# Group attentions: the first batch's mask rows taken from SBUF, not from DRAM

## The chip, the cores and the metric

One NeuronCore of a Trainium2 chip runs one program, a stack of eight layers. The metric is the device time of one execution in microseconds (us); the median of several executions is quoted. The engines are named as the profile names them: PE (TensorE), ACT (ScalarE), DVE (VectorE), POOL (GpSimd) and SP (SyncE, which issues nearly all transfers).

## The reference, cut to what matters

Eight layers work on `x` of 16 batches x 256 tokens x 128 channels. The two that matter here are the sixth and the eighth, `_L1_ffn_ref`, the "group" attention, called twice with the same weights. Every token but the first five is put into one of two groups by its likeness to a guide, and it sees only the keys of its group and the first five:

```python
sim = (sim - sim.min()) / (sim.max() - sim.min())
pos = sim > 0.9
logits = jnp.einsum('bqhd,bkhd->bhqk', q * scale, k)
def masked_attn(tok_mask):
    key_mask = jnp.concatenate([jnp.ones((Bx, REG), bool), tok_mask], axis=1)
    l = jnp.where(key_mask[:, None, None, :], logits, -jnp.inf)
    a = jax.nn.softmax(l, axis=-1)
    return jnp.einsum('bhqk,bkhd->bqhd', a, v)
x_pos = masked_attn(pos)
x_neg = masked_attn(~pos)
tok_out = jnp.where(pos[:, :, None, None], x_pos[:, REG:], x_neg[:, REG:])
```

`sim.min()` and `sim.max()` go over all 4096 tokens. So no token's group is known before all tokens have been looked at: the masks of every batch come out at once, at the end of a stage of its own.

## The kernel before, in words

A batch is 256 tokens: `NT` = 2 tiles of 128 (`P`). There are `NB` = 16 batches, so 32 tiles (`TILES`), and 16 heads in 8 pairs (`PAIRS`).

**The two stages of a group layer.** `groups` finds the groups. While it runs, SP already carries out the first pieces of the attention that follows (`following.first`): the constant rows (`sp_first`) and the query and key parts of batches 0 and 1 (`HOSTED` = 2), which go from SBUF to `stack_dram` and from there into the stacks. The last thing `groups` does is to write `K.mask`, 128 partitions x 4 kinds x 32 tiles, on DVE. Then comes a barrier, and `narrow_attention`'s `run` starts its own block.

**The stacks.** `st` holds, for three batches in turn (`KEEP`), for queries (`which` = 0) and keys (`which` = 1), for each pair and each of 256 tokens, a column of numbers along the partitions: 48 rows of bf16 parts of q and k, then at `ROW_EXTRA` two mask rows, then three rows for the maxima. One head of a pair lies in partitions 0 to 63, the other in 64 to 127 (`z`). A product of a query column with a key column gives the score with its mask already added, since a query's mask rows hold 0 or -1e30 and a key's 0 or 1. The mask rows are the same for all pairs.

**How the masks get there.** PE transposes `K.mask` (line 1007), so that kind and tile run along the partitions; ACT copies the result to `mask_rows` (line 1169). Partition 32 * a + n holds kind a of tile n. SP writes all of it to `mask_dram` (line 942), waits until that has landed (semaphore `kept0`), and issues 16 transfers at line 956 (`sp_masks`): for batch 0 and 1, for each half of the pairs (`i`), for each `z` and each `which`, one transfer of 2 rows x 4 pairs x 256 tokens, 512 bytes per row and pair. The masks of batches 2 to 15 are read in the same way by four transfers each, before each half of the stack's load (line 984).

**Who waits.** The pieces of a batch are walked through in an order written out by hand (`NARROW_ORDER`), one list an engine. On PE a batch begins with the piece "max": four matmuls a pair (line 1068) give all the scores, and DVE takes their maximum (line 1281). For the first pair and the fifth, PE waits for the masks of that half (`masked`, at 64 = four transfers of 16) and for the stack's load (`landed`). "reg_scores" (lines 1142 and 1143) waits for the first half's masks too. The pieces "score" (line 1089), "value" (line 1109) and so on follow; for batch 0 they start when all eight maxima of the batch are there.

Of the kernel before, what the change touches and what calls it, by code (L numbers as in the profile page):

```python
# [12 lines left out]
P = 128  # L13
NB = 16
S = 256
NT = S // P
TILES = NB * NT
# [571 lines left out]
PAIRS = H // 2  # L589
# [186 lines left out]
HOSTED = 2  # L776
# [39 lines left out]
def narrow_attention(nc, K, kind, name, W):  # L816
# [9 lines left out]
    ROW_EXTRA = PARTS * D8  # L826
# [11 lines left out]
    with ExitStack() as ctx:  # L838
        ctx.enter_context(nc.cleanup_on_exit())

        def sb(n, shape, dt=F32):
# [3 lines left out]
            "stat_dve", "var_ready", "rstd_ready", "norm_ready", "first_dve", "first_var", "first_rstd", "first_norm",  # L845
            "weights", "set_pe", "set_act", "set_pool", "kept0", "kept1", "rows",
            "xn", "full0", "full1", "drained0", "drained1",
            "rotated", "summed", "part", "parted0", "parted1", "landed00", "landed01", "landed10", "landed11", "masked00", "masked01", "masked10", "masked11", "pool_own", "dve_own",
            "maxima", "maxed", "joined", "split", "shifted0", "shifted1", "spread0", "spread1",
            "scored", "exps", "valued", "taken", "biased", "added", "stats",  # L850
            "reg_q", "reg_v", "reg_max", "reg_sum", "reg_new", "reg_probs", "reg_out")}
# [4 lines left out]
        masked = [s["masked00"], s["masked01"], s["masked10"], s["masked11"]]  # L856
# [7 lines left out]
        st = sb("st", [P, KEEP, 2, PAIRS, S], BF16)  # L864
# [74 lines left out]
        def sp_setup(sp):  # L939
            if kind == "group":  # L940
                sp.wait_ge(s["set_act"], 1)
                sp.dma_start(K.mask_dram.rearrange("a n p -> (a n) p"), mask_rows[:]).then_inc(s["kept0"], 16)

            for b in range(HOSTED if kind == "group" else 0):
                for i in range(2):
                    sp_masks(sp, b, i)

        def sp_masks(sp, b, i):
            half = slice(i * PAIRS // 2, (i + 1) * PAIRS // 2)
            if b == 0:  # L950
                sp.wait_ge(s["kept0"], 16)
            for z in range(2):
                at = slice(64 * z + ROW_EXTRA, 64 * z + ROW_EXTRA + 2)
                for which in range(2):
                    src = K.mask_dram[2 * which:2 * which + 2, NT * b:NT * b + NT, :].rearrange("a n p -> a (n p)")
                    sp.dma_start(st[at, b % KEEP, which, half], src.unsqueeze(1).to_broadcast([2, PAIRS // 2, S])
                                 ).then_inc(masked[2 * i + b % 2], 16)
# [65 lines left out]
        def pe_piece(pe, what, i, b):  # L1023
# [27 lines left out]
            elif what == "max":  # L1051
# [3 lines left out]
                        pe.wait_ge(s["weights"], 1)  # L1055
                        wait(pe, s["set_act"], {"slope": 1, "group": 1, "rope": 2}[kind])
                if i % (PAIRS // 2) == 0:
                    if kind == "group":
                        pe.wait_ge(masked[2 * (i // (PAIRS // 2)) + b % 2], 64 * (b // 2 + 1))
                    pe.wait_ge(landed[b % 2][i // (PAIRS // 2)], LANDED * (b // 2 + 1))  # L1060
                wait(pe, s["maxed"], PAIRS * b + i - (1 if b == 0 else 0))
                Mx = max_bank(i, b)
# [58 lines left out]
            elif what == "turnmax":  # L1121
                pe.wait_ge(s["split"], b + 1)
                for t in range(NT):
                    ins = pe.transpose(bank[0:48].bitcast(BF16)[:, t * P:(t + 1) * P],  # L1124
                                       cols[:, b % 2, t].rearrange("p r z j -> p (r z j)"), K.ident16[:])
                ins.then_inc(full[m], 1)
            elif what == "attn":
                for k in ("turn0", "turn1"):
                    pe.wait_ge(drained[fill[k, b][0]], fill[k, b][1])
                for t in range(NT):  # L1130
                    ins = pe.transpose(bank[:, t * P:(t + 1) * P], att[:, b % 2, t, :], K.ident[:])
                ins.then_inc(full[m], 1)
            elif what == "project":
                pe.wait_ge(drained[fill["attn", b][0]], fill["attn", b][1])
                for t in range(NT):
                    ins = pe.matmul(bank[:, t * C:(t + 1) * C], att_t[:, b % 2, t * P:(t + 1) * P], W["out"], start=True, stop=True)  # L1136
                ins.then_inc(full[m], 1)
            elif what == "reg_scores":
                pe.wait_ge(s["reg_q"], b + 1)
                pe.wait_ge(landed[b % 2][0], LANDED * (b // 2 + 1))  # L1140
                pe.wait_ge(masked[b % 2], 64 * (b // 2 + 1))
                pe.matmul(bank[0:RH, 0:S], qblk[:, b % 2, :], qk[:, b % 2, 1, :], start=True, stop=False)
                pe.matmul(bank[0:RH, 0:S], K.not_first[0:ROW_SHIFT, :], st[0:ROW_SHIFT, b % KEEP, 1, 0, :], start=False,
                          stop=True).then_inc(full[m], 1)
            elif what == "reg_turn":
                pe.wait_ge(s["reg_probs"], b + 1)
                for t in range(NT):
                    ins = pe.transpose(bank[:, t * RH:(t + 1) * RH], pxn[:, t * P:(t + 1) * P], K.ident[0:RH, 0:RH])  # L1148
                ins.then_inc(full[m], 1)
            elif what == "reg_value":  # L1150
                pe.wait_ge(drained[fill["reg_turn", b][0]], fill["reg_turn", b][1])
                pe.wait_ge(s["reg_v"], b + 1)
                for t in range(NT):
                    ins = pe.matmul(bank[:, 0:RH], vplain[:, t, :], pxt[:, t * RH:(t + 1) * RH],  # L1154
                                    start=(t == 0), stop=(t == NT - 1))
                ins.then_inc(full[m], 1)
# [1494 lines left out]
```

## Time and profile before

| | |
|---|---|
| median of 3 runs | 2233.96 us (2232.46 to 2238.82) |
| the profiled execution, its own time | 2238.64 us |
| its span, first to last instruction | 2236.9 us |
| mean granted TensorE clock | 0.944 of full speed |
| busy: PE, DVE, ACT, POOL | 88%, 69%, 52%, 36% of the span |
| first group layer's attention: mask write issued, first maxima | 1582.49 us, 1587.15 us |
| second group layer's attention: the same | 1957.06 us, 1961.09 us |

The span leaves out what lies before the first and after the last instruction (1.7 us here). The profile is one execution, and this one was among the slower; a difference of two of its times is more to be trusted than the sum. "Landing" of a transfer is the moment at which its semaphore has its full count; "issue" is the time that SP spends on it.

### The profile page before, as it was taken

The page shows a single profiled execution, that of the slowest core. Times are in us where ns is not written, and L with a number is a line of the kernel's source. Part 1 is how long each engine was busy: PE and PEld are TensorE (multiplying, and loading weights), DVE is VectorE, ACT ScalarE, POOL GpSimd, SP SyncE. Part 2 cuts the span into 40 slices and gives each one's busy share as a digit, 9 for nine tenths or more (in the row PEclk, how much of TensorE's full clock was granted, in tenths as well). Part 3 has the DMA queues.
Part 4 walks back from the last instruction along what each step waited for, and adds up shares of the span by engine and source line. Part 5 has one row for each costly group of instructions (what it writes and reads, how often), then busy time and mean ns, then how long its engine had stood idle before and what let it go on. Part 6 is the DMA issues. An engine that isn't in the chain of part 4 may idle for free. (4 is left out here: it accounts for less than half of the span.)

```text
span 2236.9 us, 54582 instructions
## 1 busy us (share of the span) xinstructions
PE 1978.6 (88%) x21591; PEld 1310.0 (59%) x21591; DVE 1550.5 (69%) x2798; ACT 1169.8 (52%) x1966; POOL 797.7 (36%) x1306
## 2 busy tenths in 40 slices
PE   5999999999989997999799979997599985479996
PEld 2666666666668884665588856664255542335553
DVE  5787868777876336667663367774689966779994
ACT  4444444444333324666433236666388875458874
POOL 4444544545432212343322134430333414333340
PEclk9999999999999997999899989998699997779998
DMA  6000000000013343443122524440334410224431
GB/s 175 1 1 1 2 1 1 2 1 2 2 35 70 88 106 85 122 113 96 37 64 66 127 72 116 119 109 6 94 112 115 111 48 0 58 77 108 118 110 51
DMA packets 163151, 146.71 MB, mean 66 GB/s; under 512 B 15264, under 2 KB 131376, under 8 KB 160852
## 3 DMA queue, kind: packets, MB, share of 16 engines
q1 hardware_dynamic: 162900, 143.22, 25.1%
q8 instruction: 175, 2.87, 0.6%
q14 instruction: 76, 0.62, 0.1%
HBM read 88.64 MB, written 54.52 MB: 64 GB/s over the span
## 5 line engine op out<-in xcount | busy, mean ns | idle before, releaser
L1281 DVE TENSOR_REDUCE l_group_mx<-maxima 128x4 f32<-128x1024 f32 x248 | 304.0, 1226 | 53.5 <-PE maxima L1068 51.9
L1206 ACT ACTIVATE l_group_pr<-scores 128x1024 f32<-128x1024 f32 x256 | 261.6, 1022 | 70.4 <-PE scores L1089 67.9
L2482 POOL TENSOR_TENSOR l_wide_tiles_sum<-l_wide_pr 128x256 f32<-128x256 f32 x256 | 180.9, 727 | 200.2 <-ACT l_wide_pr L2421 200.0
L2451 DVE RECIPROCAL l_wide_rc<-bank 128x256 f32<-128x256 f32 x128 | 224.0, 1750 | 5.3 <-PE bank L2378 3.8
L2421 ACT ACTIVATE l_wide_pr<-scores 128x512 f32<-128x512 f32 x256 | 139.0, 595 | 160.3 <-PE scores L2361 160.3
L2435 DVE TENSOR_REDUCE l_wide_mx<-maxima 128x2 f32<-128x512 f32 x248 | 159.3, 685 | 44.3 <-PE maxima L2341 44.1
L1281 DVE TENSOR_REDUCE l_slope_mx<-maxima 128x6 f32<-128x768 f32 x124 | 119.0, 959 | 67.9 <-PE maxima L1075 66.5
L2411 ACT ACTIVATE l_wide_qk<-bank 128x512 f32<-128x512 f32 x128 | 76.4, 597 | 155.4 <-PE bank L2325 155.4
L1281 DVE TENSOR_REDUCE l_rope_mx<-maxima 128x6 f32<-128x768 f32 x124 | 118.8, 958 | 45.1 <-PE maxima L1075 44.1
L1206 ACT ACTIVATE l_slope_pr<-scores 128x768 f32<-128x768 f32 x128 | 103.5, 809 | 74.4 <-PE scores L1096 74.3
L1109 PE MATMUL bank<-l_group_pr,va 128*32 128x256 f32 x2048 | 142.4, 397 | 0.0
L2372 PE MATMUL bank<-l_wide_pr,l_wide_va 128*64 128x256 f32 x1024 | 138.0, 390 | 2.5 <-DVE l_wide_att_t L2452 2.4
L1206 ACT ACTIVATE l_rope_pr<-scores 128x768 f32<-128x768 f32 x128 | 103.8, 811 | 66.1 <-PE scores L1096 65.9
L2361 PE MATMUL scores<-l_wide_qk 64*128 64x256 f32 x1024 | 131.4, 376 | 0.0
L1068 PE MATMUL maxima<-l_group_st 50*128 50x256 bf16 x992 | 101.6, 285 | 25.6 <-DVE l_group_mx L1281 15.2
L2477 POOL CAST l_wide_qk<-l_wide_qk 128x512 bf16<-128x512 f32 x128 | 78.1, 610 | 122.0 <-ACT l_wide_qk L2411 121.9
L1089 PE MATMUL scores<-l_group_st 53*128 53x256 bf16 x1024 | 102.4, 279 | 16.5 <-ACT l_group_pr L1206 11.7
L1379 POOL CAST l_group_cols<-l_group_mx 128x32 bf16<-128x32 f32 x32 | 6.7, 209 | 303.5 <-DVE l_group_mx L1281 303.5
L2361 PEld LDWEIGHTS scores<-l_wide_qk 64*128 64x128 f32 x1024 | 98.6, 189 | 9.8
L2372 PEld LDWEIGHTS bank<-l_wide_pr,l_wide_va 128*64 128x64 f32 x1024 | 63.3, 136 | 48.3 <-issue 21.7
L1929 ACT ACTIVATE l_rope_e_ht<-maxima 128x512 f32<-128x512 f32 x64 | 38.0, 595 | 96.6 <-PE maxima L1876 96.6
L1929 ACT ACTIVATE l_slope_e_ht<-maxima 128x512 f32<-128x512 f32 x64 | 38.0, 595 | 93.9 <-PE maxima L1876 93.9
(584 smaller groups left out, 4681.5 us busy)
## 6 DMA issues: line engine op xcount, KB each, us to landing
l_group_st<-stack_dram SPq DMA_DIRECT2D x128, 192.0 KB, 3.4
l_slope_st<-stack_dram SPq DMA_DIRECT2D x64, 192.0 KB, 4.0
l_rope_st<-stack_dram SPq DMA_DIRECT2D x64, 192.0 KB, 4.1
stack_dram<-l_group_parts SPq DMA_DIRECT2D x64, 192.0 KB, 2.3
l_slope_e_unit_prob<-prob_dram SPq DMA_DIRECT2D x16, 512.0 KB, 7.3
l_rope_e_unit_prob<-prob_dram SPq DMA_DIRECT2D x16, 512.0 KB, 7.5
stack_dram<-l_group_parts SPq DMA_DIRECT2D x64, 128.0 KB, 1.9
stack_dram<-l_slope_parts SPq DMA_DIRECT2D x32, 192.0 KB, 2.4
```

Of the source, the lines that this page charges most:

```text
L1068: ins = pe.matmul(Mx[:, z, first:first + keys], st[at, b % KEEP, 0, i, t * P:(t + 1) * P], st[at, b % KEEP, 1, i, 0:keys], start=(t == 0 o ...
L1089: ins = pe.matmul(Tp[:, z, t * S:t * S + S - first], st[at, b % KEEP, 1, i, t * P:(t + 1) * P], st[at, b % KEEP, 0, i, first:S], start=(t ...
L1109: ins = pe.matmul(Ob[i // 2][32 * z:32 * z + 32, (i % 2) * S + first:(i % 2) * S + S], va[:, b % KEEP, t, h // G, :], pr[:, (h // 2) % AHE ...
L1206: act.activation(pr[:, i % AHEAD, :, 0:keys], Tp[:, :, 0:keys], ACT.Exp).then_inc(s["exps"], 1)
L1281: dve.tensor_reduce(mx[:, b % 2, :, :, i], max_bank(i, b)[:, :, 0:BLOCKS * keys].rearrange("p z (a k) -> p z a k", k=keys), AX.X, ALU.max, ...
L2361: ins = pe.matmul(Tb[z][:, t * S:(t + 1) * S], qk[rows(z), at, i, 1, t * P:(t + 1) * P], qk[rows(z), at, i, 0, :], start=False, stop=(t == ...
L2372: ins = pe.matmul(Ob[i % 2][rows(z), 0:S], va[:, at, kt, 2 * i + z, :], pr[:, i % 2, z, kt * S:(kt + 1) * S], start=(kt == 0), stop=(kt == ...
L2421: act.activation(pr[:, i % 2, z, :], Tb[z][:], ACT.Exp).then_inc(s["exps"], 1)
L2435: dve.tensor_reduce(mx[:, at, :, 2 * i + z], max_banks(i, b)[z][:].rearrange("p (t k) -> p t k", k=S), AX.X, ALU.max, negate=True).then_in ...
L2451: own.done(dve.reciprocal(rc[:], Ob[i % 2][:, S:2 * S]))
L2477: pool.tensor_copy(qk16[:, at, i], qk[:, at, i]).then_inc(s["half"], 1)
L2482: pool.tensor_tensor(tiles_sum[:, i % 2, z, :], pr[:, i % 2, z, 0:S], pr[:, i % 2, z, S:2 * S], ALU.add).then_inc(s["added"], 1)
```

## The change

For batch 0 alone, the mask rows no longer go by way of `mask_dram`. Eight transfers read `mask_rows` in SBUF and write the stack in SBUF: for each `z`, each `which` and each of the two tiles `t`, one of 2 rows x 8 pairs x 128 tokens, 256 bytes per row and pair. They are issued right behind the write to `mask_dram`, without a wait between. Only then does SP wait for `kept0`, and issue the eight reads for batch 1. A new semaphore `masked` counts the eight transfers; PE waits for all of them (128 = 8 x 16) ahead of the first pair of batch 0, where it waited for four reads, and at the fifth pair and in "reg_scores" too. The counts expected on the old semaphores fall by one turn for the even batches. The write to `mask_dram` stays, and batches 1 to 15 read as before.

```diff
-            "rotated", "summed", "part", "parted0", "parted1", "landed00", "landed01", "landed10", "landed11", "masked00", "masked01", "masked10", "masked11", "pool_own", "dve_own",
+            "rotated", "summed", "part", "parted0", "parted1", "landed00", "landed01", "landed10", "landed11", "masked00", "masked01", "masked10", "masked11", "masked", "pool_own", "dve_own",
...
                 sp.dma_start(K.mask_dram.rearrange("a n p -> (a n) p"), mask_rows[:]).then_inc(s["kept0"], 16)
-
-            for b in range(HOSTED if kind == "group" else 0):
+                for z in range(2):
+                    for which in range(2):
+                        for t in range(NT):
+                            row, at = 64 * z + ROW_EXTRA, 2 * which * TILES + t
+                            sp.dma_start(st[row:row + 2, 0, which, :, t * P:(t + 1) * P],
+                                         mask_rows[at:at + TILES + 1:TILES, :].unsqueeze(1).to_broadcast([2, PAIRS, P])).then_inc(s["masked"], 16)
+                sp.wait_ge(s["kept0"], 16)
                 for i in range(2):
-                    sp_masks(sp, b, i)
+                    sp_masks(sp, 1, i)
 
         def sp_masks(sp, b, i):
             half = slice(i * PAIRS // 2, (i + 1) * PAIRS // 2)
-            if b == 0:
-                sp.wait_ge(s["kept0"], 16)
...
                 if i % (PAIRS // 2) == 0:
-                    if kind == "group":
-                        pe.wait_ge(masked[2 * (i // (PAIRS // 2)) + b % 2], 64 * (b // 2 + 1))
+                    if kind == "group" and b == 0:
+                        pe.wait_ge(s["masked"], 128)
+                    elif kind == "group":
+                        pe.wait_ge(masked[2 * (i // (PAIRS // 2)) + b % 2], 64 * (b // 2 + b % 2))
...
-                pe.wait_ge(masked[b % 2], 64 * (b // 2 + 1))
+                if b == 0:
+                    pe.wait_ge(s["masked"], 128)
+                else:
+                    pe.wait_ge(masked[b % 2], 64 * (b // 2 + b % 2))
```

The order of SP's instructions at the start of the first group attention, before. A name in brackets is that of the first user of a semaphore that several layers share: `rows_turned` is here the signal that `mask_rows` is there, `rows_kept` is `kept0`.

```order
L1536 UNCONDITIONAL_BRANCH
L1495 UNCONDITIONAL_BRANCH [waits barrier_Pool_Activation_PE_DVE_SP_release]
L942 DMA mask_dram<-l_group_mask_rows 128x128 [waits rows_turned]
L956 DMA l_group_st<-mask_dram 2x4x256 [waits rows_kept]
L956 DMA l_group_st<-mask_dram 2x4x256 x3
L956 DMA l_group_st<-mask_dram 2x4x256 [waits rows_kept]
L956 DMA l_group_st<-mask_dram 2x4x256 x11
L991 DMA shift_dram<-l_group_rows 48x256 [waits l0_wide_exps]
```

And the same place in the changed kernel:

```order
L1544 UNCONDITIONAL_BRANCH
L1503 UNCONDITIONAL_BRANCH [waits barrier_Pool_Activation_PE_DVE_SP_release]
L942 DMA mask_dram<-l_group_mask_rows 128x128 [waits rows_turned]
L947 DMA l_group_st<-l_group_mask_rows 2x8x128 x8
L959 DMA l_group_st<-mask_dram 2x4x256 [waits rows_kept]
L959 DMA l_group_st<-mask_dram 2x4x256 x7
L994 DMA shift_dram<-l_group_rows 48x256 [waits l0_wide_exps]
```

The wait for the write stood ahead of the first transfer that PE needs; now it stands behind all those that PE needs for batch 0. The number of transfers is 17 both times. The second group layer has the same two pieces, and on the other engines no instruction changes its place.

## Rows read from the trace of the kernel before

**Rows 1.** The page: busy time of PE, and the granted clock in 40 slices.

```profile
PE 1978.6 (88%) x21591; PEld 1310.0 (59%) x21591; DVE 1550.5 (69%) x2798; ACT 1169.8 (52%) x1966; POOL 797.7 (36%) x1306
PEclk9999999999999997999899989998699997779998
```

**Rows 2.** The chain that ended last, second group layer: start us, us, what.

```profile
1957.06 1.55 DMA mask_dram<-l_group_mask_rows
...
1958.63 0.23 SPq L956
...
1959.50 1.35 DMA l_group_st<-mask_dram
1960.85 0.25 issue
1961.09 0.62 PE maxima L1068 x4
```

**Rows 3.** Timeline of the first group layer: start, us, engine, line, operation, count [idle before].

```profile
1582.49 0.34 SPq L942 DMA_DIRECT2D mask_dram<-l_group_mask_rows  x1
...
1584.69 4.75 SPq L956 DMA_DIRECT2D l_group_st<-mask_dram  x16
...
1587.15 0.61 PE L1068 MATMUL maxima<-l_group_st 50*128 50x256 bf16 x4 [4.99 <-DMA l_group_st<-mask_dram]
```

**Rows 4.** Source views of lines 942 and 956: durations ns min/median/max, first and last start; landing.

```profile
L942 SPq DMA_DIRECT2D mask_dram<-l_group_mask_rows x2: 337/338/338, 1582.5 to 1957.1; - x2
DMA to landing us min/median/max: 1.6/1.9/2.2
L956 SPq DMA_DIRECT2D l_group_st<-mask_dram x256: 230/259/367, 1584.7 to 2181.3; - x128
  PE maxima L1068: 9.4, 2
```

**Rows 5.** Transfers in a window: 1957.85 to 1958.40 (the mask write; slices of 13.75 ns).

```profile
DMA  0000366579999776542210000000000000000000
DMA packets 145, 0.03 MB, mean 60 GB/s; under 512 B 145, under 2 KB 145, under 8 KB 145
q1 hardware_dynamic: 145, 0.03, 27.4%
```

**Rows 6.** The same for 1585.4 to 1592 (the 16 mask reads of the first layer).

```profile
DMA packets 160, 0.07 MB, mean 10 GB/s; under 512 B 32, under 2 KB 160, under 8 KB 160
q1 hardware_dynamic: 160, 0.07, 3.4%
```

**Rows 7.** The same for 1954 to 1957 (batch 1's stack loads).

```profile
DMA packets 387, 0.69 MB, mean 231 GB/s; under 512 B 48, under 2 KB 48, under 8 KB 387
q1 hardware_dynamic: 387, 0.69, 91.6%
```

**Rows 8.** Timeline of the second group layer: SP's other transfers, and batch 1's first maxima.

```profile
1944.25 1.74 SPq L984 DMA_DIRECT2D l_group_st<-stack_dram  x4
...
1952.84 1.74 SPq L984 DMA_DIRECT2D l_group_st<-stack_dram  x4
...
1958.63 4.76 SPq L956 DMA_DIRECT2D l_group_st<-mask_dram  x16
...
1973.49 0.61 PE L1068 MATMUL maxima<-l_group_st 50*128 50x256 bf16 x4 [0.59 <-DVE l_group_mx L1281]
...
1975.58 0.32 SPq L991 DMA_DIRECT2D shift_dram<-l_group_rows  x1
```

**Rows 9.** Busy time in stretches: PE, PEld, DVE, ACT, POOL (count), PEclk, DMA share, GB/s.

```profile
1577.00:1587.00 10.00, 0.84 (x3) 0.59 (x3) 1.87 (x10) 2.32 (x4) 1.51 (x5) 0.50 0.37 90
1600.00:1614.00 14.00, 10.28 (x67) 4.42 (x65) 10.07 (x13) 4.88 (x8) 5.24 (x9) 0.50 0.45 110
2000.00:2100.00 100.00, 97.38 (x1097) 53.07 (x1089) 89.89 (x152) 81.28 (x121) 38.88 (x76) 1.00 0.42 114
```

**Rows 10.** Landing of the stack loads (line 984): min/median/max.

```profile
DMA to landing us min/median/max: 2.8/3.8/5.5
```

## The prediction

> **What bounds the kernel now.** The page comes first [rows 1]: PE is busy for 88% of the span, and its clock was granted nearly in full except in a few slices. A change of some small transfers can therefore count only where PE stands still. The chain of waits of the second group layer says where that is [rows 2]: the reader is to see that the write of the masks to DRAM, one issue after another of the reads at line 956, and the landing of the fourth read follow each other with nothing beside them, and that PE's first four maxima start 0.24 us after that landing. The timeline of the first group layer shows the same stretch [rows 3], and the source view of line 956 puts 9.4 us of PE's idle time down to these transfers, in two waits [rows 4]. (Part of those waits is time before the masks were written; only what follows line 942 is in play.) From the issue of the write to the first maxima it is 1587.15 - 1582.49 = 4.66 us in the first layer and 1961.09 - 1957.06 = 4.03 us in the second. These 8.7 us are all that the change touches, 0.39% of 2238.64 us. About 0.3%, or 6.7 us, is what a measurement of this kernel can tell from no change, so a clear gain would need three quarters of the whole stretch.
>
> **The parts of the stretch before.** Second layer [rows 2]: the write is issued at 1957.06 and has landed at 1958.61; the first read starts at 1958.63, 1.57 us after the write's issue. The fourth read, the last that PE needs, starts at 1959.50, 0.87 us later. It lands 1.35 us after its issue, and PE starts 0.24 us on. 1.57 + 0.87 + 1.35 + 0.24 = 4.03. First layer [rows 3]: 2.20 us to the first read. The 16 issues take 4.75 us, 0.297 us each, so the fourth starts 3 x 0.297 = 0.89 us later, and from there to PE's start it is 1587.15 - 1584.69 - 0.89 = 1.57 us (1.35 + 0.24 = 1.59 in the other layer).
>
> **Term 1, the wait for the write goes.** The first direct transfer can be issued when SP has done the write's issue: 0.34 us [rows 4] and the 0.05 us that lies between two issues (the pitch of 0.297 less some 0.24 of issue). So it starts 0.39 us behind the write where the first read started 1.57 or 2.20 us behind it: -1.18 us in the second layer, -1.81 us in the first.
>
> **Term 2, PE needs eight transfers where it needed four.** The old split by halves of the pairs let PE start on the first four reads. The new split is by tile, and a transfer carries all eight pairs; PE waits for all eight. Four more issues at 0.297 us: +1.19 us in each layer. The issue of this form, SBUF to SBUF, stands in no row. The nearest are the mask reads, 0.230 to 0.367 us [rows 4], and the mask write, 0.34 us; with the gap a pitch of 0.28 to 0.42 us. I keep 0.297, because the new transfers have the reads' two partitions and much the same count of pieces. Over the seven pitches the ends are -0.1 and +0.9 us a layer.
>
> **Term 3, the landing of the last one.** A read's pieces: 160 packets in the window of 16 reads, 10 each, 8 of 512 bytes and two small ones [rows 6]; 3.4% of 16 engines over 6.6 us is 3.6 us, or 22 ns a packet. The write was 128 pieces of 256 bytes and some 16 small ones, one for each engine; 27.4% of 16 engines over 0.55 us is 2.4 us, or 17 ns for each of 145 [rows 5]. Two small packets a read then mean two engines. A direct transfer has 16 pieces of 256 bytes and two small ones, 18 x 17 = 0.30 us of engine time, 0.15 us on each of two engines. That is half the pitch of the issues: the eight do not pile up, and the last one's landing is that of a single transfer. For it I take the read's 1.35 us, because it too ends in SBUF; difference 0. The ends: a write's first packet stands at 1957.89, 0.84 us after its issue (the first busy slice is the fourth of 13.75 ns [rows 5]), and with 0.15 us of pieces nothing shown excludes a landing after 1.0 us, -0.35 us a layer; the slowest small transfer here landed after 2.2 us [rows 4], +0.85 us a layer.
>
> On a transfer's fixed cost the two sources differ. The rows have 1.35 us for the read, 1.55 and 2.20 for the write. The Trainium skill ("DMA: Bandwidth & Descriptors", section "Anatomy of one DMA", written for transfers that GpSimd issues) gives each a fixed 2.0 us or so. By it the removed wait would be 2.0 us in both layers, so that each gains 2.0 - 0.39 - 1.19 = 0.42 us and the estimate for both is -0.84 us.
>
> **Edits that cost nothing, and their cover.** Batch 1's eight reads are issued behind the direct ones, from 2.77 us after the write (the write has landed by then in both layers) to about 5.1 us after it; before, SP was through at 1963.39, 6.3 us after [rows 8]. Batch 1's maxima begin at 1973.49, and SP's next transfer at 1975.58, so ten microseconds cover them; without that cover a late mask would hold PE by its own landing, 1.35 us. The fifth pair of batch 0 and "reg_scores" find `masked` full. The stack loads of batch 0 were issued from 1944.25 and those of batch 1 from 1952.84 [rows 8]; they land in 5.5 us at most [rows 10], so the first is no hidden second wait at 1961, and the direct transfers, whose first packet would come at 1957.06 + 0.39 + 0.84 = 1958.3, hardly meet the second. What is late next, if the masks came at once, is the copy of `mask_rows` itself, outside the stretch. The changed counts on `masked00` and its kin ask for the same transfers. The one new semaphore costs no instruction that waits.
>
> **What carries to the end.** Up to 1614 the granted clock is 0.50, half of 2.4 GHz, from before the wait on, and PE and DVE are busy 10.3 and 10.1 of 14 us, handing to one another [rows 9]; later PE is busy 97 of 100 us. Nothing in between has a fixed time to wait for, so a start that is earlier ends earlier by as much. I put nothing for the clock: the half clock begins long before this stretch and outlasts it.
>
> **The sum.** First layer -1.81 + 1.19 + 0 = -0.62 us. Second layer -1.18 + 1.19 + 0 = +0.01 us. Together -0.6 us: 2238.64 becomes 2238.0. The profiled execution was 4.7 us over the median of the runs, 2233.96; on that median the forecast is **2233.4 us**. With the ends of terms 2 and 3 it is between -0.6 - 0.2 - 0.7 = -1.5 and -0.6 + 1.8 + 1.7 = +2.9 us.
>
> **The rivals.**
>
> *The write's 2.20 us was chance, and nothing is gained.* The forecast's gain stands on that one wait. In the second layer the same write took 1.55 us, and there the four issues added eat what the wait removed gives. If an ordinary execution has 1.57 in both, the sum is 0.0 us, 2234.0. For it: nothing in the program makes the two layers differ. Against it: one landing in two is slow.
>
> *The fixed cost of 2.0 us.* As a mechanism here: every write to DRAM takes what the first layer's nearly took, so both layers gain. With 2.20 in both by the row, 2 x -0.62 = -1.2 us, 2232.7. Against it: the second layer's 1.55. Either way far inside 0.3%.
>
> *Slower: the small pieces set the pace.* The place is the two engines' queues, between the first direct transfer and the eighth. If a piece took what one took in the stack loads, 91.6% of 16 x 3 us over 387 packets, 114 ns [rows 7], a transfer would hold its engines for 9 x 0.114 = 1.02 us. The last would land 0.39 + 0.84 + 8 x 1.02 + 0.45 after the write's issue (0.45: the write's last packet at 1958.16 [rows 5], its landing at 1958.61), and PE start at 10.1 us where it started at 4.03 and 4.66: +6.1 and +5.4, together +11.5 us, 2245.5. It begins to cost from 0.297 / 9 = 33 ns a piece, and from about 80 ns it would show as slower by 0.3%. Against it: pieces of 256 bytes out of SBUF took 17 ns, pieces into these partitions 22 ns. The Trainium skill ("DMA: Bandwidth & Descriptors", "Specifications") says that below 512 bytes the transfer engines read, modify and write, which speaks against the new pieces, half as long as the old ones; it has no factor. Its section "Why small descriptors are slow (HBM only)" excepts SBUF to SBUF. No row here shows that kind of transfer.
>
> *The change does not do what it says.* PE would have to be held by something else at that point. The chain names the masks and the other conditions are met earlier, so I give it nothing of its own; it would read as no change.
>
> **How the numbers follow.** Forecast -0.6 us with its ends: 0.74. Nothing gained: 0.15. Both writes slow: 0.04. Small pieces set the pace: 0.03. The program's code and semaphore numbers shift elsewhere and move something by more than the runs scatter: 0.04, of which 0.02 faster, 0.01 slower, 0.01 within. Faster by over 0.3%: 0.02. Slower by over 0.3%: 0.03 + 0.01 = 0.04. Within 0.3%: 0.94. The runs shown lie from 2232.46 to 2238.82, ten times the effect. The range takes the lowest with the best end, 2232.46 - 1.5 = 2231.0, and the highest with the forecast, 2238.82 - 0.6 = 2238.2, which holds the median with the dearest end too (2236.9).
>
> **What would show it.** In the changed profile: eight transfers at line 947, each issued in 0.23 to 0.34 us, the first 0.39 us behind the write; PE's first maxima 4.0 to 4.1 us behind the write in both layers, the wait put down to the direct transfers; batch 1's reads through about 5.1 us behind it. Term 1 is wrong if SP stands still between line 942 and 947. Term 2 is wrong if the eight take other than 2.4 us. Term 3 is wrong if PE starts other than 1.6 us after the eighth's issue. The carry is wrong if the first maxima move and the end of the layer does not move with them. The whole is wrong if the median leaves the range.

## The result, and the profile after

The changed kernel took 2240.08 us (median of 20 runs, 2236.72 to 2243.57), the kernel before 2235.45 us (20 runs, 2232.46 to 2238.82). The ratio is 1.0020, 95% interval 1.0014 to 1.0026: 3.1 to 5.8 us slower. That is less than 0.3%, as forecast, but 2240.08 lies above the range given, and the sign is not that of the forecast of -0.6 us. On the median of the kernel before that stood beside it, 2235.45, the forecast would have been 2234.8. The profiled execution took 2240.27 us, with a span of 2238.6 us.

The page of the changed kernel has the same instruction counts and the same clock in each slice as [rows 1]:

```profile
PE 1980.8 (88%) x21591; PEld 1312.3 (59%) x21591; DVE 1549.3 (69%) x2798; ACT 1169.5 (52%) x1966; POOL 797.2 (36%) x1306
PEclk9999999999999997999899989998699997779998
```

The chain that ended last, second group layer (start us, us, what), answers to [rows 2]:

```profile
1956.72 0.34 SPq L942
...
1957.11 0.57 SPq L947
...
1961.13 1.66 DMA l_group_st<-l_group_mask_rows
1962.79 0.25 issue
1963.04 0.62 PE maxima L1073 x4
```

The write's landing is gone from the chain, and the first direct transfer starts 0.39 us behind the write, as the forecast had it. But one issue now takes 0.52 us (the first one 0.57) and not 0.26, and eight of them stand in a line. The first group layer shows the same in its timeline (start, duration, engine, line, count), against [rows 3]:

```profile
1580.35 0.34 SPq L942 DMA_DIRECT2D mask_dram<-l_group_mask_rows  x1
1580.74 4.66 SPq L947 DMA_DIRECT2D l_group_st<-l_group_mask_rows  x8
...
1585.45 2.54 SPq L959 DMA_DIRECT2D l_group_st<-mask_dram  x8
...
1586.80 0.61 PE L1073 MATMUL maxima<-l_group_st 50*128 50x256 bf16 x4 [6.79 <-DMA l_group_st<-l_group_mask_rows]
```

The source views (durations in ns min/median/max) put the two kinds of transfer side by side; [rows 4] has 230/259/367 for the reads of before:

```profile
L947 SPq DMA_DIRECT2D l_group_st<-l_group_mask_rows x16: 522/523/673, 1580.7 to 1961.1; - x16
...
  PE maxima L1073: 13.4, 2
...
L959 SPq DMA_DIRECT2D l_group_st<-mask_dram x240: 230/258/492, 1585.4 to 2182.2; - x120
```

PE waited 13.4 us for the direct transfers ahead of its first maxima in the two layers, where it had waited 9.4 us for the reads [rows 4]: +4.0 us. The packets in the window from 1958.2 to 1963.0 of the changed kernel, nearly all of them the direct transfers', answer to [rows 5] and [rows 6]:

```profile
DMA packets 164, 0.04 MB, mean 8 GB/s; under 512 B 156, under 2 KB 164, under 8 KB 164
q1 hardware_dynamic: 164, 0.04, 3.5%
```

3.5% of 16 engines over 4.8 us is 2.7 us, 16 ns a packet. The small pieces are as quick as they were read off [rows 5]; the transfer engines have nothing to do most of this time.

**Where the time is.** Take as the stretch what lies between PE's transposition of the masks and PE's first maxima, since nothing else is changed. Before, the transpositions of line 1007 stand in the timeline at

```profile
1581.89 0.26 PE L1007 MATMUL scores<-ident,mask 128*128 128x128 bf16 x1 [4.32 <-PEq L1536]
1956.45 0.27 PE L1007 MATMUL scores<-ident,mask 128*128 128x128 bf16 x1 [4.30 <-PEq L1536]
```

and in the changed kernel at

```profile
1579.75 0.26 PE L1010 MATMUL scores<-ident,mask 128*128 128x128 bf16 x1 [4.31 <-PEq L1544]
1956.12 0.26 PE L1010 MATMUL scores<-ident,mask 128*128 128x128 bf16 x1 [4.31 <-PEq L1544]
```

With the starts of the maxima in [rows 3] and [rows 2], the stretches were 5.26 and 4.64 us; they are 7.05 and 6.92 us. The sum rose from 9.90 to 13.97 us, by 4.07. What lies between and behind the stretches stayed: from the first layer's first maxima to the second layer's transposition it is 369.30 us before and 369.32 us after, from the second layer's first maxima to the end of the span 275.8 and 275.6. What was added there came out at the end in full. The two spans differ by only 1.7 us because the changed kernel's execution came to its first transposition 2.14 us earlier. That part of the program is the same, and the six variants below reached it between 1576.7 and 1580.9 us, so this is scatter between executions and no effect of the change.

### The profile page after: what moved, and what is told of

Read it like the earlier page. It is cut to its first block and busy times, and to the rows that moved or that the text cites. A ratio compares the mean times of both kernels' runs of the same rounds, so it can differ in the third digit from the quotient of the medians.

```text
span 2238.6 us, 54582 instructions
## 1 busy us (share of the span) xinstructions
PE 1980.8 (88%) x21591; PEld 1312.3 (59%) x21591; DVE 1549.3 (69%) x2798; ACT 1169.5 (52%) x1966; POOL 797.2 (36%) x1306
```

## The experiments

In the table, a stretch is as above, read from the trace of each kernel, and the ratio is that of the run times to the kernel before, measured beside it.

| kernel | stretch, layers 1 and 2, us | sum less before's | ratio (95%) |
|---|---|---|---|
| before | 5.26, 4.64 | | |
| changed | 7.05, 6.92 | +4.1 | 1.0020 (1.0014 to 1.0026) |
| same eight shapes, read from DRAM | 6.53, 6.21 | +2.8 | 1.0012 (0.9997 to 1.0027) |
| write issued behind the eight | 6.64, 6.57 | +3.3 | 1.0011 (0.9997 to 1.0025) |
| four direct transfers | 5.74, 5.64 | +1.5 | 1.0009 (1.0000 to 1.0018) |
| four direct, on two queues | 4.27, 4.03 | -1.6 | 0.9999 (0.9990 to 1.0008) |
| four DRAM reads, on two queues | 5.70, 4.56 | +0.4 | 1.0003 (0.9994 to 1.0011) |
| eight direct, on two queues | 5.46, 5.17 | +0.7 | 1.0007 (0.9998 to 1.0016) |

The ratios of the six variants do not by themselves tell one from no change (0.1% is 2.2 us, and each interval is about as wide as that to either side). They run in the order of the stretches, near enough; the stretches are what the verdicts below rest on. How far these scatter is seen in the three probe kernels below, which hold the kernel before's own program: from the write's issue to the first maxima their sums over the two layers are 8.9, 9.0 and 9.1 us, where the kernel before has 8.7. Where the write is waited for, a difference of 0.4 us in the sum therefore tells nothing.

**The same shapes from DRAM.** The eight transfers read `mask_dram` behind the wait for the write:

```diff
+                sp.wait_ge(s["kept0"], 16)
+                from_dram = K.mask_dram.rearrange("a n p -> (a n) p")
...
-                                         mask_rows[at:at + TILES + 1:TILES, :].unsqueeze(1).to_broadcast([2, PAIRS, P])).then_inc(s["masked"], 16)
-                sp.wait_ge(s["kept0"], 16)
+                                         from_dram[at:at + TILES + 1:TILES, :].unsqueeze(1).to_broadcast([2, PAIRS, P])).then_inc(s["masked"], 16)
```

> The changed kernel with its eight transfers in the same shapes, but read from mask_dram behind the wait for the write. Theory A (SBUF on both sides costs the issue): issues of 0.26 to 0.28 us, pitch 0.30; PE's first maxima 1.57 to 2.2 + 7 x 0.30 + 1.6 = 5.3 to 5.9 us behind the write's issue; 1.2 us a layer more than the kernel before, +2.4 us in all, ratio to before 1.001. Theory B (the shape costs): issues of 0.52 us, pitch 0.57, first maxima 7.5 to 8.1 us behind the write, +6.8 us in all, ratio 1.003.

Measured, in the source view of that kernel:

```profile
L949 SPq DMA_DIRECT2D l_group_st<-mask_dram x16: 231/263/265, 1583.3 to 1960.1; - x16
```

and in its chain, the last read and its landing:

```profile
1960.11 1.38 DMA l_group_st<-mask_dram
```

The issue is 0.263 us with the same 16 pieces of 256 bytes, the same destination and the same repeats. First maxima stood 1586.99 - 1581.07 = 5.92 and 1961.73 - 1956.12 = 5.61 us behind the write's issue. So the shape is not what costs; what changed is that the source lies in SBUF. The run also measures term 2 alone: it has the kernel before's issue and landing, and eight transfers to wait for instead of four. From the first read's issue to the first maxima it took 3.73 and 3.72 us, where the kernel before took 2.46 in both layers, so four more reads cost 1.26 us a layer. The rest of the +2.8 us is a write that landed 0.3 us later in the second layer.

**The write behind the eight.** Only the line of the write is moved:

```diff
-                sp.dma_start(K.mask_dram.rearrange("a n p -> (a n) p"), mask_rows[:]).then_inc(s["kept0"], 16)
                 for z in range(2):
...
+                sp.dma_start(K.mask_dram.rearrange("a n p -> (a n) p"), mask_rows[:]).then_inc(s["kept0"], 16)
                 sp.wait_ge(s["kept0"], 16)
```

> The changed kernel with the write to mask_dram issued behind the eight direct transfers instead of ahead of them. Theory (the eight issues are the path, one behind the other): the first maxima 7 x 0.57 + 1.66 + 0.25 = 5.9 us behind the first direct issue, so 0.39 us a layer less than the changed kernel, 0.8 us in all; issues still 0.52 us. Rival (the direct transfers are slow because they share the engines with the write just issued, whose landing rose from 1.6 or 2.2 to 2.2 or 2.4 us): issues fall to 0.26 us and the landing to 1.35, first maxima about 3.7 us behind the first direct issue, 2.6 us a layer less than the changed kernel.

The source view:

```profile
L946 SPq DMA_DIRECT2D l_group_st<-l_group_mask_rows x16: 522/523/672, 1581.5 to 1960.6; - x16
```

and the landing of the last direct transfer in the chain:

```profile
1960.56 1.69 DMA l_group_st<-l_group_mask_rows
```

The issues are unchanged, so the write that is still under way does not slow them. First maxima 6.04 and 5.96 us behind the first direct issue; 0.76 us less than the changed kernel's stretches in sum, as the 0.39 us a layer had it.

**Which forms are dear.** The kernel before with small transfers added at its end, ahead of the store of the result; the program's own work is untouched, and nothing it reads later is written. Three transfers of a form, to different places, then a wait. Each figure below rests on three issues in one execution:

```python
for n, r in enumerate((16, 48, 112)):
    sp.dma_start(landing[r:r + 2, :, 0:P], source[0:33:32, 0:P].unsqueeze(1).to_broadcast([2, PAIRS, P])).then_inc(probed, 16)
settle()
```

> The kernel before, and at its end, ahead of the store of the result, 13 forms of small transfer on SP, three of each to different rows or columns, each three waited for: (1) the old mask read, DRAM to SBUF, 2 x 4 x 256; (2) 2 x 8 x 256; (3) the new form's shape from DRAM; (4) the new form itself, SBUF to SBUF, rows 32 partitions apart, 128 elements repeated 8 times; (5) with adjacent rows; (6) with 4 repeats; (7) 8 repeats of 256 elements; (8) 4 repeats of 256; (9) one piece of 128 a row, no repeat; (10) 8 different pieces of 128; (11) one run of 2048 a row; (12) 128 partitions of 128; (13) SBUF to DRAM, 2 rows of 128. The source of the probes is a tile of zeros. Theory A (SBUF on both sides is what costs; the run from DRAM in the same shape had issues of 0.263 us where the direct ones have 0.523): (4) to (12) all about 0.5 us, (1) to (3) 0.26, (13) 0.25 to 0.34. Theory A2 (SBUF on both sides costs by the piece): (9) 0.28, (6) and (8) 0.39, (4) 0.52, (12) far over 0.52. Theory C (the step of 32 partitions): (5), (10), (11) and (12) 0.26 to 0.34, (4) and (6) to (9) 0.5. Landing after the end of an issue: about 1.1 us for all of 2 rows.

The source views, for (1), (4), (5), (8), (9) and (13) in this order, as ns min/median/max:

```profile
L2637 SPq DMA_DIRECT2D landing<-mask_dram x3: 236/252/253, 2223.7 to 2224.3; - x3
L2646 SPq DMA_DIRECT2D landing<-source x3: 522/555/686, 2229.7 to 2231.0; - x3
L2649 SPq DMA_DIRECT2D landing<-source x3: 622/633/680, 2232.7 to 2234.1; - x3
L2658 SPq DMA_DIRECT2D landing<-source x3: 523/523/523, 2241.5 to 2242.6; - x3
L2661 SPq DMA_DIRECT2D landing<-source x3: 472/492/514, 2244.3 to 2245.4; - x3
L2673 SPq DMA_DIRECT2D mask_dram<-source x3: 248/253/254, 2256.2 to 2256.8; - x3
```

Every transfer from SBUF to SBUF is at 0.47 us or above, one single piece a row too; the others have medians of 0.25 to 0.27. (12), with 128 pieces, has a median of 0.60, and (7), with twice the bytes of (4), 0.52. So neither the number of pieces nor the bytes are what costs (theory A2), and neither is the step of 32 partitions: adjacent rows, (5), are dearer still.

**Which sides.**

> The kernel before, and at its end 13 more forms on SP, three of each: (1) two rows of 128 from DRAM to DRAM; SBUF to SBUF with one piece of 128 a row: (2) one row, same partition, (3) one row from a partition 8 on, (4) two rows, same partitions, (5) to (9) two rows whose sources lie 2, 8, 16, 32, 64 partitions apart, (10) step 8 on both sides; (11) DRAM to two rows 8 partitions apart; (12) 16 rows, SBUF to SBUF; (13) 16 rows from DRAM. Theory A (an issue is dear when both sides are SBUF; in the run of forms before, 0.49 to 0.66 us for all nine of those and 0.25 to 0.27 for the DRAM ones): (2) to (10) and (12) 0.45 to 0.66, (1), (11), (13) 0.25 to 0.30. Theory D (an issue is cheap when the sides are of unlike kind): (1) 0.5 too. The source's step decides only within 0.49 to 0.66.

Theory A held for the SBUF to SBUF forms (0.47 to 0.68 us) and fell with the others; theory D has (1) right and falls with (11). The source views for (1), (5), (11), (12) and (13):

```profile
L2637 SPq DMA_DIRECT2D mask_dram<-mask_dram x3: 544/582/583, 2224.9 to 2226.1; - x3
L2649 SPq DMA_DIRECT2D landing<-source x3: 563/563/563, 2236.7 to 2237.9; - x3
L2667 SPq DMA_DIRECT2D landing<-mask_dram x3: 541/552/552, 2252.8 to 2254.0; - x3
L2670 SPq DMA_DIRECT2D landing<-source x3: 541/585/588, 2255.7 to 2256.9; - x3
L2673 SPq DMA_DIRECT2D landing<-mask_dram x3: 336/417/420, 2258.6 to 2259.5; - x3
```

DRAM to DRAM is as dear, and so is DRAM to two rows that lie 8 partitions apart.

**Controls.**

> The kernel before, and at its end 13 forms on SP, three of each. In the run of sides before this one, a transfer from DRAM to two rows 8 partitions apart took 0.54 us to issue and DRAM to DRAM 0.58, so that 'both sides in SBUF' is not the whole of it. In order: (1) DRAM to two adjacent rows, one piece of 128 each; (2) the same to rows 8 apart; (3) to rows 8 apart with 8 repeats; (4) SBUF to DRAM from two adjacent rows; (5) from rows 8 apart; (6) from rows 32 apart; (7) DRAM to one row; (8) DRAM to 16 rows; (9) the old mask read, 2 x 4 x 256; (10) the new direct form; (11) the old read again; (12) DRAM to DRAM; (13) the old read again. Theory E (cheap, 0.25 to 0.34, is only a transfer with exactly one side in SBUF and its partitions adjacent): (1), (4), (7), (8), (9), (11), (13) cheap; (2), (3), (5), (6), (10), (12) 0.47 to 0.6. Theory F (one piece a row is dear, a repeated one cheap, when the other side is DRAM): (1), (2), (7) dear and (3), (9) cheap. Theory G (it is the place in the program or what was issued before): (9), (11) and (13) differ.

The source views for (2), (4), (5), (6), (8), (9) and (12):

```profile
L2640 SPq DMA_DIRECT2D landing<-mask_dram x3: 541/576/687, 2230.9 to 2232.3; - x3
L2646 SPq DMA_DIRECT2D mask_dram<-source x3: 235/247/257, 2237.1 to 2237.7; - x3
L2649 SPq DMA_DIRECT2D mask_dram<-source x3: 542/567/622, 2238.7 to 2240.0; - x3
L2652 SPq DMA_DIRECT2D mask_dram<-source x3: 452/467/467, 2241.6 to 2242.6; - x3
L2658 SPq DMA_DIRECT2D landing<-mask_dram x3: 312/415/418, 2245.8 to 2246.6; - x3
L2661 SPq DMA_DIRECT2D landing<-mask_dram x3: 241/254/261, 2248.3 to 2248.9; - x3
L2670 SPq DMA_DIRECT2D mask_dram<-mask_dram x3: 584/585/589, 2255.1 to 2256.3; - x3
```

Theory E sorts all of them. (3) and (10) were dear with 0.59 and 0.52 us, (1), (7), (11) and (13) cheap with 0.25 to 0.26. The one that it has slightly wrong is (8): 16 rows from DRAM cost 0.42, more than 0.34. It makes the direct form of the change dear for two reasons, either of which would do: both sides lie in SBUF (adjacent rows do not help, (5) of the first probes), and the source rows are stepped (they cost 0.47 towards DRAM too, (6) here). Theory F falls with (1) and (3), theory G with (9), (11) and (13), which agree while dear forms stand between them. Why a stepped row or a second side in SBUF costs some 0.3 us of issue is not shown by any run; nor why two rows 32 or 64 partitions apart come at 0.47 to 0.49 and rows 1 to 16 apart at 0.56 to 0.62.

**Four direct transfers.** The masks are turned by two transpositions so that a batch's two tiles lie in one row of 256:

```diff
+                for t in range(NT):
+                    ins = pe.transpose(Tp[0:4 * NB, 0, :].bitcast(BF16)[:, t * P:(t + 1) * P],
+                                       K.mask[:].rearrange("p a (b t) -> p t (a b)", t=NT)[:, t, :], K.ident16[:])
...
+                        row, at = 64 * z + ROW_EXTRA, 2 * which * NB
+                        sp.dma_start(st[row:row + 2, 0, which],
+                                     mask_rows[at:at + NB + 1:NB, :].unsqueeze(1).to_broadcast([2, PAIRS, S])).then_inc(s["masked"], 16)
```

> The masks are turned so that both tiles of a batch lie in one row (two transposes instead of one, 64 rows of 256 columns), and batch 0 takes four direct transfers of 2 rows x 8 pairs x 256 instead of eight of 128. Theory A (each direct issue costs 0.52 us, pitch 0.57, whatever its piece count): four in 2.3 us, the first maxima 0.39 + 3 x 0.57 + 1.66 + 0.25 = 4.0 us behind the write's issue, 2.3 us a layer less than the changed kernel, and some 0.15 us later to the write for the second transpose and the longer copy; against the kernel before -0.6 + 0 + 0.3, so ratio 1.000, and against the changed kernel 4 us less. Theory A2 (by the piece or the byte): the issue rises to 0.6 us or more, and the gain shrinks.

The first maxima came 4.91 and 4.81 us behind the write, not 4.0. In the source view:

```profile
L946 SPq DMA_DIRECT2D l_group_st<-l_group_mask_rows x8: 622/624/807, 1578.1 to 1954.7; - x8
```

and in the chain:

```profile
1954.65 1.92 DMA l_group_st<-l_group_mask_rows
```

The write's issue rose to 0.47 and 0.52 us, an issue to 0.62, the landing to 1.92. The dearer issue is not theory A2's price by the byte, since (7) of the first probes, the same pieces at a step of 32, had 0.52; its rows are 16 partitions apart, and in the probes such a step cost 0.08 us more than one of 32 (0.562 against 0.487). The landing, from the end of the issue, is 1.30 us; in the probes (7), also of 8 KB, landed 1.3 us behind the end of its last issue and (4), of 4 KB, 1.1 us. Half the transfers took 2.6 us off the two stretches, of 4 us expected; it still does not reach the kernel before.

**Four direct ones on two queues.** As the last, but SP issues the two of the lower partitions, ahead of the write, and ACT those of the upper ones:

```diff
+                act.wait_ge(s["set_act"], 1)
+                for which in range(2):
+                    row, at = 64 + ROW_EXTRA, 2 * which * NB
+                    act.dma_start(st[row:row + 2, 0, which],
+                                  mask_rows[at:at + NB + 1:NB, :].unsqueeze(1).to_broadcast([2, PAIRS, S])).then_inc(s["masked"], 16)
```

> As the last, but the two direct transfers of the upper partitions are issued by ACT right behind its copy of the mask rows, and SP issues its two ahead of the write to mask_dram. Theory (the path is: so many issues one behind the other, then one landing): first maxima 1 x 0.57 + 1.66 + 0.25 = 2.5 us behind the first direct issue, where the kernel before has 4.03 and 4.66 behind the write: 1.5 and 2.2 less, less 0.15 each for transpose and copy, -3.3 us in all, ratio 0.9985. ACT's later work (two activations and a table load, 2.1 us, wanted 4.5 us after the first maxima) hides its 1.2 us of issues. Rival (two queues' transfers hold one another up on the same engines, or an issue from ACT costs more): first maxima later than 3.5 us, ratio 0.9995 or above.

The chain, second layer:

```profile
1954.96 0.69 SPq L945
...
1955.70 2.21 DMA l_group_st<-l_group_mask_rows
...
1958.16 0.63 PE maxima L1074 x4
```

The chain of the second layer shows one issue where there were four or eight, and a landing of 2.21 us where 1.66 was expected. The first maxima came 3.4 and 3.2 us behind the first issue, not 2.5, though earlier than the rival's 3.5. Both things that the rival names are there in part: an issue from ACT took 0.63 to 1.25 us, and the ratio is where it put it, above 0.9995. The stretches are 5.7 us shorter than the changed kernel's and 1.6 us shorter than the kernel before's; the run time beats the changed kernel's (0.9990 to 1.0008 against 1.0014 to 1.0026) and is not told apart from the kernel before's.

**Eight direct ones on two queues.** The changed kernel's own transfers, four issued by SP behind the write, four by ACT:

```diff
+                act.wait_ge(s["set_act"], 1)
+                first_masks(act, 1)
...
-                for z in range(2):
+                first_masks(sp, 0)
```

> The changed kernel with its eight direct transfers shared out: SP issues its four behind the write, ACT the other four behind its copy of the mask rows. Nothing else is changed. Theory (it is the line of eight issues that holds PE): first maxima 0.39 + 3 x 0.57 + 1.66 + 0.25 = 4.0 us behind the write, 2.3 us a layer less than the changed kernel, -4.6 us in all: ratio to the kernel before 1.000. Rival (the direct transfers themselves, or their piling up on two engines, hold PE): 6 us and ratio 1.002 as with eight on one queue.

The stretches fell by 3.3 us in sum, of 4.6 expected; the first maxima stood 4.86 and 4.57 us behind the write. The transfers, their shapes, their number and the two sides are those of the changed kernel. Only the line of issues is halved, and with it goes most of what was lost (3.3 of 4.1 us). What falls short of the 4.6 stands in the chain, as the landing of the last one, and in the source view of ACT's issues:

```profile
1958.50 2.09 DMA l_group_st<-l_group_mask_rows
...
L943 ACTq DMA_DIRECT2D l_group_st<-l_group_mask_rows x8: 533/670/1140, 1581.5 to 1958.1; - x8
```

**Four DRAM reads on two queues.** Batch 0's four reads carry all pairs; SP and ACT issue two each behind the wait for the write:

```diff
+        def first_masks(eng, z):
+            for which in range(2):
+                row = 64 * z + ROW_EXTRA
+                src = K.mask_dram[2 * which:2 * which + 2, 0:NT, :].rearrange("a n p -> a (n p)")
+                eng.dma_start(st[row:row + 2, 0, which], src.unsqueeze(1).to_broadcast([2, PAIRS, S])).then_inc(s["masked"], 16)
```

> The masks of batch 0 by way of DRAM again, as four reads with all eight pairs each (2 x 8 x 256), two issued by SP and two by ACT, both behind the wait for the write. Theory (path = write's landing, issues in a line, one landing): 1.57 to 2.2 + 1 x 0.30 + 1.38 + 0.25 = 3.5 to 4.1 us from the write's issue to the first maxima, 0.55 us a layer less than the kernel before; -1.1 us in all, ratio 0.9995, which is about as good as the direct form on two queues (ratio 0.9999) without a direct transfer. Rival: an issue from ACT is dearer, as it was for the direct ones (0.63 to 1.25 us), and nothing is gained.

The chain, second layer:

```profile
1953.73 0.23 SPq L943
...
1954.01 1.96 DMA l_group_st<-mask_dram
```

A miss: nothing is gained. The issues are as cheap as before, also from ACT (median 0.260 us, one of four at 0.56), but the last landing takes 1.96 us where one queue had 1.35 to 1.38. That rise eats the 0.6 us of issues saved: from the first read's issue to the first maxima it is 2.55 and 2.49 us, where it was 2.46. (The other 0.3 us of the +0.4 is the write, which landed after 2.55 us in the first layer.) Some 0.15 us of the rise belong to the form, twice as large: in the probes, on one queue, (2) landed 1.26 us behind the end of its last issue and (1) 1.11 us. A later landing stands in all three kernels with two queues; no run shows its cause.

## Why the prediction was wrong, point by point

- **What bounds it, and what is in play**: right. The stretch behind line 942 is all that moved.
- **Term 1, the wait for the write goes**: right to the hundredth. The first direct transfer started 0.39 us behind the write in both layers.
- **Term 2, eight transfers at the pitch of 0.297 us**: this is the step that failed. Eight instead of four was right, and the run with the DRAM source confirms the price of four more reads (1.26 us a layer, 1.19 forecast). From the first direct issue to the eighth it took 1961.13 - 1957.11 = 4.02 us in the second layer, not 2.08, which is a pitch of 0.574 us, and 0.1 us more in the first layer, where the eight issues took 4.66 us in all: +2.0 us a layer. The error was to choose the nearest rows by partitions and pieces and to pass over what no row shared: a source and a destination both in SBUF, and source rows 32 partitions apart. The dearest end, 0.42 us, was taken from the same rows of transfers with one side in DRAM, so it was no bound.
- **Term 3, the landing**: forecast 1.35 us from the issue, measured 1.66. It is the same error again. From the end of an issue it is 1961.13 + 0.52 to 1962.79, 1.14 us, where before it was 1959.50 + 0.26 to 1960.85, 1.09 us. The landing was right; the issue inside it was too short by half.
- **The sum**: with 0.39, 4.02 and 1.66 + 0.25 in the place of 0.39, 2.08 and 1.59, the second layer takes 6.32 us from the write, which is what the chain shows; the first took 6.45. Against 4.03 and 4.66 the sum is +4.1 us instead of -0.6, beyond the dearest end that the prediction gave, +2.9. The medians differ by 4.6, with an interval of 3.1 to 5.8.
- **The slower rival, small pieces**: it had the sign but not the mechanism. The packets took 16 ns, the engines were idle in between, and the queues did not pile up. The Trainium skill ("DMA: Bandwidth & Descriptors", section "Why small descriptors are slow (HBM only)") excepts transfers between SBUF and SBUF from the penalty for small pieces; by that exception, the trace agrees as far as the pieces go, with those 16 ns.
- **The 2.20 us as chance**: wrong. In the kernels that wait for the write it landed after 2.20, 2.19 and 2.55 us in the first layer and after 1.57, 1.89 and 1.47 in the second (issue to next issue, in the kernel before, in the one with eight DRAM reads and in the one with four on two queues). The three kernels with probes hold the kernel before's own program up to the probes, and have 2.26, 2.41 and 2.22 against 1.55, 1.47 and 1.85. The reason stays open, but the layer alone is not it: where the write was issued later, the layers agree (1.52 and 1.53 us behind the eight, 2.02 and 2.00 with four direct ones on two queues). The transfers of the kernel before from 1582.49 to 1584.69 show one thing that only the first layer has: one packet of 8 KB on the queue that the profile calls instruction, which took some 0.5 us (1.4% of 16 engines over 2.2 us). Nine packets of the write, as many as one engine has of it, start 1.3 to 1.5 us behind the write's issue, and all others by 1.1, as in the second layer. Such a packet stands beside the write in the first layer of all nine kernels that issue it right behind the copy, and in the second layer of none. In the second layer the landing of the write in its old form went with how busy all transfers, the last stack loads among them, kept the engines meanwhile: 1.4 to 1.5 us at 10 to 13%, 1.55 to 1.57 at 27 and 28%, 1.85 to 1.89 at 31 and 38%, and 2.4 at some 50%, in the changed kernel. No run changes one of the two alone, so neither is shown to be the cause.
- **The fixed cost of 2.0 us**: the writes landed after 1.4 to 2.5 us, so no one figure holds for them, and nearly all those of the second layer were fast, so that both layers do not gain alike. The Trainium skill's fixed cost of about 2.0 us ("DMA: Bandwidth & Descriptors", section "Anatomy of one DMA", written for transfers that GpSimd issues) lies among these, and well over the 1.35 us of a small read; for both the rows decide.
- **What costs nothing**: right. Batch 1's reads were through at 1585.45 + 2.54 = 1587.99, 7.6 us behind the write and not 5.1, still eleven microseconds ahead of their use.
- **The carry and the clock**: right, one for one, and the granted clock's slices are the same. The rival of code and semaphore numbers that shift something elsewhere finds nothing: 369.30 and 369.32 us between the stretches, 275.8 and 275.6 behind them.

## What to carry to other kernels

When a transfer is priced for which no row exists, ask first which of its properties no row shares (here: both sides in SBUF, and a stepped source), and take the bound from there, not from rows that resemble it in size. A wait of one round trip of 1.6 to 2.2 us is soon bought back by a line of issues: count the issues that stand ahead of the first reader and multiply by the time from one issue to the next (0.57 us here), since that time, and not the bytes, was the path here. A detour through DRAM can be the cheaper way where it turns the dear form of issue into the cheap one.

## What the runs showed of the hardware

- In the probes, an issue on SP took 0.22 to 0.27 us for transfers of one or two adjacent partitions with the other side in DRAM, 0.31 to 0.42 for 16 of them; the mask write with its 128 partitions took 0.34 (0.40 right behind the direct ones). It took 0.45 to 0.69 us in the probes when both sides were in SBUF, when both were in DRAM, or when the rows of the SBUF side did not adjoin; in the program single ones of this kind took up to 0.81 us on SP and 1.25 on ACT. At one step, repeats and pieces (1 to 16) moved the median only between 0.49 and 0.56.
- The time from the end of such an issue to the landing was 1.1 us for both kinds on one queue, up to 4 KB, and 1.3 us for 8 KB.
- With SP and ACT issuing at the same time, the last small transfer landed 0.3 to 0.6 us later than with SP alone (2.21 against 1.92 and 2.09 against 1.66 directly; 1.96 against 1.38 from DRAM, where some 0.15 us are the larger form's).
- The write of 128 rows of 256 bytes to DRAM landed 1.4 to 2.5 us after its issue in the kernels that have it in this form.
